# A graph's adjacency matrix in 25 tiles of one-hot products instead of ten

## The reference

```python
def _gcn_conv(x, W, b, src, dst, dinv):
    xw = x @ W
    norm = (dinv[src] * dinv[dst])[:, None]
    agg = jax.ops.segment_sum(xw[src] * norm, dst, num_segments=x.shape[0])
    agg = agg + xw * (dinv * dinv)[:, None]
    return agg + b

x = x + _positional_encoding(n, x.shape[1])          # x: the layer norm's output
deg = jax.ops.segment_sum(jnp.ones_like(dst, dtype=x.dtype), dst, num_segments=n) + 1.0
dinv = deg ** (-0.5)
h = _gcn_conv(x, W1, b1, src, dst, dinv)
h = jax.nn.relu((h - mu) * jax.lax.rsqrt(var + BN_EPS) * gamma + beta)
h = jax.nn.relu(_gcn_conv(h, W2, b2, src, dst, dinv))
```

## Time and profile before

| | us |
|---|---|
| three runs, median (lowest, highest) | 1907.96 (1906.45, 1912.11) |
| the profiled execution | 1914.18 |
| its span | 1912.4 |
| first oh_src to the copy of the last adjacency tile | 19.01 to 288.75 |
| first matmul with the adjacency | 304.58 |

### The profile page before, as it was taken

How to read it: one execution, slowest core, us unless ns; L and a number is a source line. 1 busy time by engine, 2 the same in 40 slices (tenths; PEclk the granted TensorE clock), 3 DMA queues, 4 the chain that set the end, 5 groups by cost and what they waited for, 6 DMA issues and landing times.

```text
span 1912.4 us, 23516 instructions
## 1 busy us (share of the span) xinstructions
PE 1720.6 (90%) x9198; PEld 1550.3 (81%) x9198; DVE 877.9 (46%) x1562; ACT 537.5 (28%) x611; POOL 116.8 (6%) x99
## 2 busy tenths in 40 slices
PE   6988888999999998999999999999799765999996
PEld 3555557989999897898988988889799755988985
DVE  6998893522344113225334254343443545544531
ACT  6301102213321113223242233332310022444442
POOL 0011110000000000000000000000000001233221
PEclk9998998999999999999999999999999965999998
DMA  4023241103220521001011010110543274667654
GB/s 138 11 64 111 88 158 41 41 23 111 87 68 27 154 108 56 23 23 46 16 50 49 23 49 23 48 40 23 226 127 103 73 253 128 165 192 188 202 150 84
DMA packets 63521, 171.58 MB, mean 90 GB/s; under 512 B 7776, under 2 KB 28487, under 8 KB 62216
## 3 DMA queue, kind: packets, MB, share of 16 engines
q1 hardware_dynamic: 55240, 142.78, 23.1%
q0 software_dynamic: 8192, 27.53, 6.9%
HBM read 116.79 MB, written 56.93 MB: 91 GB/s over the span
## 4 chain that ended last, share of the span: by engine, by line
PE 83%; DVE 7%; ACT 5%; issue 2%; SPq 1%; DMA 1%; POOL 0%; DVEq 0%; POOLq 0%; ACTq 0%
PE slot L1280 35%; PE slot L1310 10%; PE slot L1334 10%; PE slot L1505 5%; PE slot L1515 5%; PE kvb L1387 3%; PE slot L1419 3%; PE slot L1374 3%; PE kvb L1505 2%; PE slot L1410 2%; DVE oh_dst L902 1%; PE slot L1488 1%; SPq L448 1%; PE lsb L1481 1%; DVE qp_l L1062 1%
## 5 line engine op out<-in xcount | busy, mean ns | idle before, releaser
L1280 PE MATMUL slot<-big_hi,slab_h 128*128 128x418 f32 x1152 | 289.6, 360 | 25.9 <-issue 8.8
L1280 PE MATMUL slot<-big_lo,slab_h 128*128 128x418 f32 x1152 | 286.1, 357 | 0.0
L1280 PE MATMUL slot<-big_hi,slab_l 128*128 128x418 f32 x1152 | 283.9, 355 | 0.0
L1280 PEld LDWEIGHTS slot<-big_hi,slab_h 128*128 128x128 f32 x1152 | 217.8, 191 | 36.2 <-issue 9.4
L1310 PE MATMUL slot<-oh_src,oh_dst 125*125 125x418 bf16 (+1 forms) x1068 | 222.2, 365 | 18.9 <-DVE oh_dst L902 18.8
L1280 PEld LDWEIGHTS slot<-big_lo,slab_h 128*128 128x128 f32 x1152 | 219.7, 191 | 3.3
L1280 PEld LDWEIGHTS slot<-big_hi,slab_l 128*128 128x128 f32 x1152 | 219.4, 191 | 3.5
L1310 PEld LDWEIGHTS slot<-oh_src,oh_dst 125*125 125x125 bf16 x1068 | 136.7, 143 | 103.2 <-DVE oh_dst L902 69.2
L902 DVE TENSOR_SCALAR oh_src<-iota_t,srcf 125x1250 bf16<-125x1250 f16 x356 | 194.5, 546 | 23.7 <-PE slot L1310 15.2
L1334 PE MATMUL slot<-adj,xs_h 125*128 125x418 f32 x480 | 119.8, 358 | 4.8 <-DVE xs_l L898 4.1
L1334 PE MATMUL slot<-adj,xs_l 125*128 125x418 f32 x480 | 118.6, 355 | 0.0
(11 more groups left out here) (241 smaller groups left out, 2531.0 us busy)
## 6 DMA issues: line engine op xcount, KB each, us to landing
slab_raw<-slabs_dram SPq DMA_DIRECT2D x48, 512.0 KB, 3.6
ws_raw<-w_dram SPq DMA_DIRECT2D x36, 512.0 KB, 5.6
w_raw<-w_dram SPq DMA_DIRECT2D x9, 1024.0 KB, 4.8
xs_raw<-xs_d SPq DMA_DIRECT2D x16, 560.0 KB
gnn_d<-htmp SPq DMA_DIRECT2D x8, 627.0 KB, 3.2
gnn_in<-gnn_d SPq DMA_DIRECT2D x8, 627.0 KB, 4.5
xt<-x_dram SPq DMA_DIRECT2D x10, 448.0 KB
xn_d<-xn SPq DMA_DIRECT2D x10, 448.0 KB
```

The costliest lines, as they stand in the source:

```text
L1280: mm = ten.matmul(ps[:, 512 * q:512 * q + CW], w[a][:, kt, :], big[b][:, kt, CW * q:CW * q + CW], start=(kt == 0 and c == 0), stop=(kt == ...
```

## The change

The adjacency is made in 25 tiles of DW = 50 destination nodes, and already with sources on the partitions. A source is written as 125 x high + low. The one-hot of the low part (`oh_src`, 125 x 128 for each chunk) is the weight; all four chunks of a group get theirs by one comparison of two 16-bit operands that are both broadcast. The other operand, `oh_key` (125 x 500), is one where an int16 key, 2048 x (9 - high) + destination, equals `key_iota` plus the tile's first node. It has four buffers, each named outright in the loop. One matmul of 500 columns for each chunk then yields the tile's 50 columns of all ten source blocks.

```diff
@@ vector, stage G @@
-                            dve.wait_ge(oh_used[j], r + 1)
-                            ts(oh_src[j][:, :], iota_t[:, :], srcf[:, bass.ds(c, 1)], ALU.is_equal)
-                            ts(oh_dst[j][:, :], iota_t[:, T * b:T * b + T], dstf[:, bass.ds(c, 1)], ALU.is_equal
-                               ).then_inc(oh_ready[j], 1)
+                            dve.wait_ge(oh_used[j], r + 1)
+                        tt(oh_src[:, :, :], lane[:, :].unsqueeze(1).to_broadcast([T, GC, 128]),
+                           src_16[:, bass.ds(group * GC, GC)].unsqueeze(2).to_broadcast([T, GC, 128]), ALU.is_equal)
+                        for j in range(GC):
+                            c = group * GC + j
+                            ts(oh_key[j][:, :], key_iota[:, :], float(DW * t), ALU.add, key[:, bass.ds(c, 1)],
+                               ALU.is_equal).then_inc(oh_ready[j], 1)
@@ tensor, stage G @@
-                    for to, at_, w in span:
-                        ten.matmul(ps[:T, to:to + w], zeros[:T, :T], iota_t[:, at_:at_ + w],
-                                   start=True, stop=False, skip_group_check=True)
+                    loops = shifts[:, DW * t:DW * t + T * NT].rearrange("p (j c) -> p j c", c=T)[:, :, 0:DW]
+                    unit = shifts[:, T * (NT - 1):T * NT]
+                    ten.matmul(ps[:T, 0:KW], unit, loops, start=True, stop=False, skip_group_check=True)
...
-                            for q, (to, at_, w) in enumerate(span):
-                                mm = ten.matmul(ps[:T, to:to + w], oh_dst[j][:, :], oh_src[j][:, at_:at_ + w],
-                                                start=False, stop=False, skip_group_check=True)
-                            mm.then_inc(oh_used[j], 1)
+                            ten.matmul(ps[:T, 0:KW], oh_src[:, j, 0:T], oh_key[j][:, :], start=False, stop=False,
+                                       skip_group_check=True).then_inc(oh_used[j], 1)
...
-                elif kind == "GT":
+                elif kind == "DG":
                     b = k[1]
-                    ten.wait_ge(diag_added, b + 1)
+                    ten.wait_ge(act_done, ACTED[("G", tile_after(b) - 1)])
                     for j in range(NT):
-                        mm = ten.transpose(ps[:T, 128 * j:128 * j + T], cnt[b % 2][:, T * j:T * j + T],
-                                           ident[:T, :T])
+                        mm = ten.matmul(lsb[:T, 2 * b:2 * b + 2], adj[:, j, T * b:T * b + T], ones_r[:T, :],
+                                        start=(j == 0), stop=(j == NT - 1))
@@ scalar, stage G @@
-                    copy(cnt[b % 2][:, 0:2 * CW].rearrange("p (q c) -> p q c", c=CW),
...
-                    copy(adj[:, :, T * b:T * b + T], blocks(ps, NT, T, T)).then_inc(act_done, 1)
+                    copy(adj[:, :, DW * t:DW * t + DW], ps[:T, 0:KW].rearrange("p (j d) -> p j d", d=DW)
+                         ).then_inc(act_done, 1)
@@ vector, stage ZP @@
+                    if layer == 1:
+                        dve.wait_ge(pe_landed[s_], LAND * (n // 2 + 1))
+                        tt(raw, raw, pes[s_][:, :, :], ALU.add).then_inc(xs_added, 1)
+                        dve.wait_ge(xs_added, n + 1)
```

More of the change, by code:

```diff
@@ L20 @@
 F16 = mybir.dt.float16
+I16 = mybir.dt.int16
 I32 = mybir.dt.int32
@@ L39 @@
 NG = NCH // GC
+GP = 80
+SUB = NG // GP
+DW = 50
+NDT = N // DW
+KW = NT * DW
+KEY_STEP = 2048
+ROUND_OFF = 12582912.0
 HEADS, DH, FEAT = 16, 64, 256
@@ L58, with tile_after @@
 SLAB = {k: n for n, k in enumerate(SLABS)}
+def tile_after(b):
+    return -(-T * (b + 1) // DW)
 def steps():
[L63 to L66, removed]
-            o.append(("LNS",))
[L68 to L73, removed]
+    o = [("LNA", i) for i in range(3)]
+    for t in range(NDT):
+        o.append(("G", t))
+        if t + 3 < NT:
+            o.append(("LNA", t + 3))
+        if t == NT - 3:
+            o.append(("LNS",))
+        if t >= NT - 2 and t - NT + 2 < NT:
+            o.append(("LNB", t - NT + 2))
+        o += [("DG", b) for b in range(NT) if tile_after(b) == t]
+    o += [("DG", b) for b in range(NT) if tile_after(b) == NDT]
+    o += [("DEG",), ("DB",)]
     def with_split(key):
@@ L189, in build @@
 def build(nc, x, src_cols, dst_cols, dst_groups, slabs, w1, w2, wr, proj, feat_rows, consts, group_no, tie,
-          iota, pe, blank, before, places, tokens, out):
+          iota, keys, pe, blank, before, places, tokens, out):
     ctx = ExitStack()
@@ L265, in build @@
                  for q in range(2)] for s in range(2)]
-        pet = [at(f"pet{s}", XS + 4096 * s, [T, D]) for s in range(2)]
-        x0t = [at(f"x0t{s}", XS + 8192 + 4096 * s, [T, D]) for s in range(2)]
+        pes = [at(f"pes{s}", (30112, 75136)[s], [T, NT, 128]) for s in range(2)]
         ZT = XS + 30720
@@ L342, in build @@
         xn_d = nc.dram_tensor("xn_d", [N, D], F32, kind="Internal").ap()
-        xs_d = [nc.dram_tensor(f"xs_d{i}", [KD, T, NT * 128], F32, kind="Internal").ap() for i in range(2)]
+        h_d = nc.dram_tensor("h_d", [KD, T, NT * 128], F32, kind="Internal").ap()
         gnn_d = nc.dram_tensor("gnn_d", [KD, 128, NP], F32, kind="Internal").ap()
@@ L927, in find_bounds @@
+                dve.tensor_copy(src_16[:, :], src_lo[:, :])
+                link(ts(src_hi[:, :], src_hi[:, :], -float(KEY_STEP), ALU.mult, float((NT - 1) * KEY_STEP), ALU.add))
+                link(tt(key[:, :], key[:, :], src_hi[:, :], ALU.add))
+                dve.wait_ge(const_in, 16 * 3)
+                dve.wait_ge(shifts_zeroed, 1)
+                dve.tensor_copy(shifts[:, T * (NT - 1):T * NT], ident[:T, :T]).then_inc(shifts_ready, 1)
                 dve.wait_ge(keys_max, 1)
-                lo, hi, n_, st, w = (lims[0:1, NT * i:NT * i + NT] for i in range(5))
@@ L1287, in _ @@
                 kind = k[0]
-                if kind not in PSUM_KINDS and kind not in ("KV", "S"):
+                if kind not in PSUM_KINDS and kind not in ("KV", "S", "DG"):
                     continue
```

236 lines of the change are left out of this document (121 added, 115 removed).

## The result

The changed kernel takes 1980.25 us (median of four runs, 1975.37 to 1980.80), the kernel before in the same comparison 1908.2 us. The ratio of their means is 1.0369, with a 95% interval of 1.0346 to 1.0392. It is slower by 72 us. The forecast was 1984 us in a range of 1920 to 2000.

A forecast was written before the change was run, and what follows sets the result against it. VectorE paced the adjacency (356 chunks at 0.617 us). Now 104 turns of 3.18 us at the lower clock make 331 us; with start 22.6, borders 9 and LNS 3.5, the reciprocal moves +75.8 us: 1984 us, range 1920 to 2000.

The forecast's parts named there:

- nine DG: Ten small matmuls with 125-column weights at nine tile borders: at most 2.1 us each, about 1 showing, 9 us.
- LNS: VectorE's Newton step waits until ACT has copied tile 7, loaded a table and taken the root: +3.5 us once.
- (a): Each turn's oh_src comparison, 512 elements from two tensors: between 0.35 and 0.68 us, taken as 0.68, leaving 0.60.
- (b): The turn's keys, 500 elements from int16 to bf16: 0.34 us a record, 0.26 from key to key.
- rival with slow keys: int16 not compared at the fast 16-bit rate: 1997 us at half rate, 2084 at one element a time; chance 0.08.
- (c): Links between engines in a turn: VectorE to TensorE 0.05 us, TensorE to VectorE 0.16 us.
- (d): A turn's 500-column matmuls: 0.42 us apart and 0.62 long at the lower clock, 0.21 and 0.37 at full clock.
- Which clock: TensorE in the adjacency: lower clock, 1.2 GHz, throughout, from cold start and pauses of 1.2 us each turn; 0.60.
- rival with full clock: TensorE keeps its full clock in the adjacency: 2.35 us a turn, -15.6 us, 1892 us; chance 0.13.
- Start: Before bounds_ready: casts go; ten key steps, a fifth doubling and one load come: +3.6 us, first one-hot at 22.6.
- POOL: POOL's twenty instructions go, and with them 21 us of blocked VectorE comparisons, already counted in the sum.
- End, x + encoding: The addition now on VectorE, eight times 1.48 us, hidden beside the matmuls of DB and column blocks: nothing.

The follow-up runs named there:

- the dense forms: Changed kernel, its two-operand comparison reading two dense tables, or one repeated only in the outer dimension (adjacency meaningless): 1936.95 and 1941.46 us.
- the filler run: Changed kernel plus five zero-weight matmuls of 500 columns behind the four of every turn, into a bank nobody reads: 1914.76 us, ratio 1.0029.
- crosswise ring: Changed kernel with the four one-hots interleaved, each number four times in the table, edge numbers broadcast over the outer dimension: 1952.36 us, ratio 1.0212.
- outer-broadcast form: Changed kernel, its comparison reading 128 dense elements repeated four times in the outer dimension and a dense second operand (adjacency meaningless): 1941.46 us.

## Why the prediction was right, point by point

The forecast for the profiled execution was 1990 us, the time 1980.8 us. The reciprocal moved by 68.2 us instead of 75.8. The terms of that sum, as the prediction put them:

| term | predicted | measured |
|---|---|---|
| first one-hot | 22.6 us | 18.09 us |
| a turn, lower clock | 3.18 us | 3.20 us |
| a turn, full clock | 2.35 us | 2.47 us |
| turns at the lower clock | all 104 | all but 14 |
| nine DG | 9 us | 9 x 1.30 = 11.7 us |
| LNS | 3.5 us | 8.45 - 3.20 = 5.3 us |
| other borders | 0 | 0 |
| last copy to reciprocal | 3.15 us | 3.45 us |

From the first one-hot to the last copy it is 340.3 us, where the prediction has 366.2 - 22.6 = 343.6. So -4.5 at the start, -3.3 between, +0.3 at the end: -7.5 of the 7.6 us. The -3.3 between are the turns at full clock, -9.3, against +1.6 for the turn, +2.7 for DG and +1.8 for LNS: part of the good fit is that these errors cancel.

- **(a), the comparison.** 693 ns where 0.68 us was taken; the bound of 0.35 us didn't come, and the dense forms show why.
- **(b), the keys.** The int16 comparison of 500 elements runs at the rate of the 16-bit float ones; the group's mean is 346 ns, the term was 0.34. The rival with slow keys is out:

```profile
L902 DVE TENSOR_SCALAR oh_key<-key_iota,key 125x500 bf16<-125x500 int16 x416 | 116.8, 346 | 0.0
```

- **(c) and (d).** Two errors cancel. The four matmuls take 1.93 us, not 2.03, and from their end to the next comparison it is 0.26 us, not 0.16. At full clock only the second is left, and makes 0.10 of the 0.12 us by which that turn was read too short. VectorE to TensorE was as read, 0.40 us with the key itself.
- **Which clock.** The choice that decided the sum was right, and of the reasons given the pauses (1.27 us in each turn) hold it; the start at the lower clock does not, since the filler run starts there too and leaves it by the third turn. It was not quite "throughout". Five times the clock came back for a few turns and fell again, in the ring's own full-clock form, with TensorE busy 2.79 of 6.6 us:

```profile
114.20:120.80 6.60, 2.79 (x11) 1.10 (x9) 4.51 (x13) 2.35 (x4) 0.00 (x0) 0.99 0.00 0
121.00:226.00 105.00, 69.59 (x167) 33.50 (x166) 52.97 (x157) 12.88 (x17) 0.00 (x0) 0.50 0.09 29
```

 So the ring has had its full clock five times and lost it again each time within a few turns: here too it is not the start that decides. The 14 short turns save 9.3 us. What lets the clock come back at just these places isn't settled.
- **The rival with full clock** would have given 1892 us. The run with the filler had this clock and took 1914.76 us, 23 us more. From the first comparison to the last turn's end it takes 275 us there where the rival has 253: 12.5 by the turn (2.47 for 2.35), 3 by DG (3.38 - 2.47 each), 3 by LNS (8.58 - 2.47), and 4 by the other borders and a few turns at the lower clock. The earlier start takes 5 us off, so its reciprocal starts at 296.29 us where the rival has 278; 3 us of the rest are that the kernel before took 1910.81 us in those runs. Had TensorE kept its clock, the result would have been "the same", and the 0.13 given to a gain of 15 us was for a case that was really no gain.
- **Start.** The step that failed, by 4.5 us: ten steps and a fifth doubling did come, but VectorE's first instruction, which waits for the edge list and the tables together, starts 3.9 us earlier (7.05 against 10.98 us); that the narrower tables are the cause is argued. The other 0.6 us are that the added steps cost 3.0 us instead of 3.6. The prediction counted instructions on VectorE and didn't ask when their inputs come.
- **DG and LNS** were read too small by 2.7 and 1.8 us. At DG the ten matmuls lie whole in front of the next tile's first one (2.26 us alone behind the last tile), and the cover by the comparison hides less than half of them. At LNS the prediction's own part was right (from 122.96 us, where the next comparison would have started, to the end of the Newton step at 126.63 it is 3.7 us), but it put the border at nothing there too, and behind the Newton step no matmul covers it:

```profile
126.46 0.17 DVE L899 TENSOR_TENSOR rstd<-nw 125x10 f32<-125x10 f32 x1
128.21 0.69 DVE L899 TENSOR_TENSOR oh_src<-lane,src 125x512 bf16<-125x512 f16 x1 [1.58 <-issue]
```

 These 1.58 us, in which VectorE waits for no other engine, are the rest of the 5.3 us.
- **POOL.** The 21 us that the prediction counted as a gain inside the sum are 25 us where they are taken alone, in the kernel before.
- **End, x + encoding.** As predicted; the addition stands beside the twenty matmuls of DB and is not felt:

```profile
364.38 1.48 DVE L899 TENSOR_TENSOR xs_raw<-xs_raw,pes 125x1280 f32<-125x1280 f32 x1
...
364.48 4.60 PE L1355 MATMUL slot<-diag,onesf 125*128 125x125 f32 x20 [3.23 <-DVE diag L899]
```

## What to carry to other kernels

Merging instructions also merges their waits. Four comparisons in one saved 0.05 us a turn, and the common wait that came with it, with the clock that it took along, cost 1.57 us a turn (3.26 against 1.69 for the same four comparisons): merge up to the point where the other engine still has a buffer in hand. When a pair of engines takes turns, add the ring's steps one after another at both clocks of TensorE, and ask which clock its pauses leave it; a pause of 1.3 us in each 3.2 us kept it at half in 90 of 104 turns. And a broadcast operand of 16 bits should be laid so that the step within is one: that was worth 28 us here, some 7 of them through the clock, for a change of two access patterns and a table, and 15 us with the ring open (1853.16 to 1838.58 us).

## What the runs showed of the hardware

- Additional matmuls without use made the changed kernel 65 us faster (1980.25 to 1914.76 us), through the granted clock (a turn of 2.47 instead of 3.20 us).
- TensorE's clock stayed at the lower of its levels (0.50, 1.2 GHz) over 105 us with its records filling 69.59 us (66%) in bursts of 1.93 us, and it was at full (2.4 GHz) with 46.79 of 50 us filled. The 63% of the earlier trace rows at full clock was no guide: busy share alone doesn't tell the clock.
- A two-operand 16-bit comparison of 512 elements takes 693 ns if one operand has step zero within, and 425 ns if the zero step is in the outer dimension or nowhere. At 256 elements it is 419 and 289 ns.
- A one-operand comparison with int16 input takes 346 ns for 500 elements, in line with 323 ns for 420 and 546 ns for 1250 of 16-bit floats.
- Weights that TensorE reads with a step of 8 B cost next to nothing over dense ones: three loads in 0.72 us against 0.70 us, at the lower clock.
- VectorE's comparison starts 0.26 us behind the matmul it waits for when its operand's address comes from a register, and 0.13 us when the addresses are fixed. The crosswise ring (0.26 us) differs from the outer-broadcast form (0.13 us) in this and in the tables read, so the register is the likely cause; no run changed it alone.
